# A gated attention block and a routed expert layer in one kernel: routing a block sooner, norms on ScalarE, and a new order of the start

## The reference

```python
x = layernorm(x0)                       # x0: (8, 512, 128), float32; no scale, eps 1e-5
# attention: a second layernorm (with ln_w, ln_b), then
uv = silu(xn @ uv_w.T + uv_b)           # u: 256, v: 256, base: 128 columns
q, k = rope(base * gamma[i] + beta[i])  # i = 0, 1
kern = square(relu(q @ k.T / sqrt(128) + w[j - i + 63]))   # index clipped to 0..126
attn = (u * (kern @ v)) @ o_w.T + o_b + x
# expert layer on x, N = 4096 rows, 8 experts, top 2
probs = sigmoid(x @ W_router); top-2, weights normalised to sum 1
ffn = sq_relu(x @ W_sh_up) @ W_sh_down + sum_e combine[:, e] * (sq_relu(x @ W_up[e]) @ W_down[e])
out = x0 + attn + ffn
```

## Time and profile before

| | |
|---|---|
| median of 3 runs | 433.27 us (432.76 to 434.15) |
| profiled execution | 432.69 us, of it 430.5 us span |
| mean granted clock of TensorE | 0.954 of full speed |
| PE / DVE / ACT / POOL busy | 369.2 / 238.2 / 227.2 / 151.2 us |
| turns 0 to 6 end on PE | 222.3 us |
| first send, last send landed | 139.4, 239.4 us |
| slot tiles on PE | 241.8 to 400.6 us |
| turn 7 and final sums | 401.1 to 430.5 us |

### The profile page before, as it was taken

The page is one execution under the profiler, slowest core; times in us unless marked ns, Lnnn a source line. Parts: engine busy times, 40 slices in busy tenths (PEclk is TensorE's granted clock), DMA queues, the critical chain, the costliest instruction groups (busy, mean ns, idle before and its releaser), DMA issues.

```text
span 430.5 us, 7290 instructions
## 1 busy us (share of the span) xinstructions
PE 369.2 (86%) x1970; PEld 280.1 (65%) x1971; DVE 238.2 (55%) x622; ACT 227.2 (53%) x421; POOL 151.2 (35%) x150
## 2 busy tenths in 40 slices
PE   1557899999899879989950499999999999999992
PEld 1345468676465636646520399999999999999840
DVE  3668877377988858758440133333333333333677
ACT  0354373675466635576520176666666666666520
POOL 3005220000000776764677024444444444444300
PEclk9989899999999998999995599999999999999997
DMA  6929800000000122146111112121212221211397
GB/s 142 266 71 273 177 0 2 1 0 2 0 0 2 45 68 94 46 131 203 45 50 50 50 46 70 56 68 56 68 56 68 56 68 50 74 56 43 108 293 210
DMA packets 50310, 34.00 MB, mean 79 GB/s; under 512 B 5876, under 2 KB 46708, under 8 KB 50293
## 3 DMA queue, kind: packets, MB, share of 16 engines
q1 hardware_dynamic: 43538, 23.71, 21.9%
q0 software_dynamic: 4352, 8.99, 6.3%
q10 hardware_dynamic: 2402, 1.10, 1.1%
HBM read 17.83 MB, written 15.95 MB: 78 GB/s over the span
## 4 chain that ended last, share of the span: by engine, by line
PE 44%; issue 23%; DMA 13%; POOL 8%; DVE 3%; ACT 0%; DVEq 0%; ACTq 0%; SPq 0%
PE bank L1269 15%; DMA slots_in<-work,slot_i 12%; POOL slots_in L982 8%; PE bank L1250 8%; PE bank L1004 5%; PE bank L1005 5%; PE bank L1006 5%; PE bank L1105 3%; PE bank L1243 2%; PE bank L1091 1%; DVE x_all L810 1%; DVE x_all L808 1%; PE bank L1068 1%; DMA slot_x<-slots_in 1%; PE bank L1040 0%
## 5 line engine op out<-in xcount | busy, mean ns | idle before, releaser
L982 POOL DMA_INDIRECT slots_in<-work,slot_i x64 | 68.0, 1062 | 113.8 <-issue 93.3
L991 POOL DMA_INDIRECT results<-work,dest x72 | 69.3, 963 | 95.8 <-DVE work L919 93.0
L1269 PEld LDWEIGHTS bank<-wdn,work 128*128 128x128 f32 x576 | 75.1, 191 | 6.0
L1269 PE MATMUL bank<-wdn,work 128*128 x576 | 75.7, 274 | 0.0
L919 DVE TENSOR_SCALAR work<-bank,row_sum 128x128 f32<-128x128 f32 x72 | 25.2, 350 | 84.0 <-PE bank L1269 82.1
L1105 PE MATMUL bank<-kern,v 128*128 128x512 f32 x128 | 60.3, 606 | 0.0
L592 ACT ACTIVATE work<-bank 128x512 f32<-128x512 f32 x72 | 43.3, 601 | 16.2 <-PE bank L1250 16.0
L598 ACT ACTIVATE work<-bank 128x512 f32<-128x512 f32 x72 | 43.1, 598 | 8.5 <-PE bank L1006 3.1
L586 ACT CAST sx_hi<-bank 128x128 fp32r<-128x128 f32 x72 | 19.0, 266 | 48.5 <-PE bank L1243 48.1
L1250 PE MATMUL bank<-cst,work 128*128 128x128 f32 x288 | 43.9, 275 | 0.0
L1105 PEld LDWEIGHTS bank<-kern,v 128*128 128x128 f32 x128 | 23.5, 197 | 22.0 <-issue 22.0
(11 more groups left out here) (162 smaller groups left out, 657.7 us busy)
## 6 DMA issues: line engine op xcount, KB each, us to landing
slots_in<-zeros SPq DMA_DIRECT2D x1, 4752.0 KB, 22.5
slot_x<-slots_in SPq DMA_DIRECT2D x36, 132.0 KB
work<-in_L_ffn_W_up SPq DMA_DIRECT2D x8, 256.0 KB, 3.1
wdn<-in_L_ffn_W_down SPq DMA_DIRECT2D x4, 512.0 KB, 7.4
wup_hi<-results SPq DMA_DIRECT2D x8, 256.0 KB, 5.1
wup_lo<-results SPq DMA_DIRECT2D x8, 256.0 KB, 5.2
out<-x_all SPq DMA_DIRECT2D x8, 256.0 KB, 3.1
results<-work,dest POOLq DMA_INDIRECT x72
```

What stands on the lines that cost most here:

```text
L982: pool.indirect_dma_start(slots_in, bass.IndirectOffsetOnAxis(slot_i[:, k, t:t + 1], 0), xs1[:, t, at], None, element_offset=k * 2).then_i ...
L991: pool.indirect_dma_start(results, bass.IndirectOffsetOnAxis(dest[:, at:at + 1], 0), slot_y[:, k, :], None).then_inc(returned[k], 16)
L1269: last = pe.matmul(P_Y[h][:, 0:D], hid_t[:, h, rows], wdn[:, of, c, :].rearrange("p a d -> p (a d)"), start=(c == 0), stop=(c == HC - 1))
```

## The change

- The routing's groups 1 to 4 are turned in turn 0 and 5 to 7 in turn 1, logits 0 to 3 in turn 0 and 4 to 7 in turn 1; the DVE pieces each stand one turn earlier (`routing_first`, `_second`, `_weights` in turn 1, `_counts`, `_tiles`, `_slots` in turn 2, `_owners` in turn 3).
- The norms of groups 1 to 7 are 28 activations on ACT (`norm`, with `shift` = -mean x inverse made on POOL) in place of 28 DVE operations. DVE keeps the norm of group 0.
- W_up is split two experts a turn in turns 3 to 6.
- `rotate_sum` of the next block stands at the end of a turn, ahead of `gate`, and not behind it.
- The start: DVE norms block 0 ahead of the uv-bias work, the first rows' parts come ahead of the second's on ACT, and on PE the gates and shared products of block 0 stand ahead of its value part; `output_weights` comes later. SP's loads stand in another order and take over the four small column loads from ACT's queue.
- The score bias: `w` is loaded to 128 partitions, POOL's four copies work on 128 partitions in place of one, 128 equal rows (512 KB) go to DRAM, and the readback starts one element less far in each row, so that it needs neither matmuls nor ACT's copies.

```diff
-            sp.dma_start(w_sb[:, :], w.rearrange("(a n) -> a n", a=1)).then_inc(ld["w"], 16)
+            sp.dma_start(w_sb[:, :], w.rearrange("(a n) -> a n", a=1).broadcast_to([P, WREL])).then_inc(ld["w"], 16)
             load_rows(0, 0, FIRST)
-            load_rows(1, FIRST, 12)
...
+            load_rows(1, FIRST, 12)
+            cols(uvb_c[:, 0:2], uv_b[0:EU].rearrange("(a p) -> p a", p=P))
...
+            sp.dma_start(cos_sin[:, :, :], consts[:, C_COS:C_W].rearrange("p (a t) -> p a t", a=2)).then_inc(ld["cos_sin"], 16)
             sp.dma_start(vb_bc[:, :], uv_b[EU:2 * EU].rearrange("(a e) -> a e", a=1).broadcast_to([P, EU])).then_inc(ld["wide"], 16)
+            load_rows(2, 12, 20)
             sp.wait_ge(ld["dist"], 16)
-            sp.dma_start(bias_t[:, :], bass.AP(by_distance.tensor, by_distance.offset, [[1, P], [1, BIAS_W]])).then_inc(ld["bias"], 16)
+            shifted = bass.AP(by_distance.tensor, by_distance.offset + P - 1, [[2 * T - 1, P], [1, BIAS_W]])
+            sp.dma_start(bias_t[:, :], shifted).then_inc(ld["bias"], 16)
...
+            def norm(g):
+                act.wait_ge(shift_made, {1: 1, 2: 2, 3: 2, 4: 2}.get(g, 3))
+                for t in range(g * TB, g * TB + TB):
+                    last = act.activation(xs1[:, t, X0:X0 + D], x_all[:, t, :], ACT.Identity, bias=shift[:, t:t + 1], scale=inv1[:, t:t + 1])
+                last.then_inc(xs1_act, 1)
...
 (ACT, turn)
+                if 3 <= route < LAST:
+                    weights_hi(2 * route - 5)
+                    weights_hi(2 * route - 4)
                 shared_relu(b, 2)
                 shared_relu(b, 3)
+                if route == 0:
+                    norm(1)
+                    norm(2)
+                    routing_copied(1)
                 if not last:
                     second_rows_hi(b + 1)
...
 (DVE, turn)
                 if 0 < b < LAST:
                     gate(b - 1)
-                if not first:
-                    rotate_sum(b)
-                    v_bias(b)
+                v_bias(b)
                 qk_split(b)
...
                 if route == 1:
-                    first_norm(6)
-                    first_norm(7)
+                    routing_first()
                 if route == 2:
-                    routing_first()
+                    routing_counts()
                 if route == 3:
-                    routing_counts()
-                if route == 4:
                     routing_owners()
...
                 if not last:
                     rotate_base(b + 1)
                     first_rows_lo(b + 1)
+                    rotate_sum(b + 1)
...
 (POOL)
+            pool.wait_ge(var_made, 3)
+            root(inv1, var_eps, slice(FIRST, 8))
+            mean_shift(slice(FIRST, 8), 3)
+            pool.wait_ge(var_made, 4)
+            root(inv2, inv2, slice(FIRST, 8))
+            root(inv1, var_eps, slice(8, 20))
+            mean_shift(slice(8, 20), 5)
```

More of the change, by code:

```diff
@@ L814, in turn @@
                     gate(b - 1)
-                if not first:
-                    rotate_sum(b)
-                    v_bias(b)
+                v_bias(b)
                 qk_split(b)
                 if route == 0:
-                    variances(slice(FIRST, 20))
-                    dve.wait_ge(bias_kept, 2)
-                if route == 1:
-                    first_norm(5)
+                    statistics(2, 12, 20)
+                    dve.wait_ge(ld["bias"], 16)
                 kernel_square(b, 0)
@@ L826, in turn @@
                 if route == 0:
-                    first_norm(1)
-                if not last:
+                    variances(slice(FIRST, 20))
+                elif not last:
                     second_norm(b + 1)
@@ L1026, in value_bias @@
                 pe.matmul(banks[6][:, 0:EU], lnb_bc, uvt_v, start=True, stop=True).then_inc(uv_bias_mm, 1)
-            def score_bias():
-                pe.wait_ge(ld["cst"], 16)
-                pe.wait_ge(ld["bias"], 16)
-                pe.wait_ge(ow_made, 1)
-                for n in range(2):
-                    pe.matmul(banks[4 + n][:, 0:BIAS_W // 2], cst[:, C_REV:C_REV + P],
-                              bias_t[:, n * (BIAS_W // 2):(n + 1) * (BIAS_W // 2)], start=True, stop=True).then_inc(bias_turned, 1)
             def routing_logits(g):
@@ L1135, in turn, with gates, first_up @@
             def turn(b, first, last, route):
+                def gates():
+                    uv_part("u0", b, 0)
+                    uv_part("u1", b, P)
+                def first_up():
+                    pe.wait_ge(x1_lo_made, START + b + 1)
+                    if first:
+                        pe.wait_ge(w_lo_made, 1)
+                    shared_up(b, 0)
+                    if route == 1:
+                        routing_turned(6)
+                    shared_up(b, 1)
+                if first:
+                    gates()
+                    first_up()
                 v_part(b, 0)
@@ L1178, in turn @@
                     output_turned(b - 1)
+                if first:
+                    pe.wait_ge(ow_made, 1)
                 values(b, 0)
+                if route == 0:
+                    routing_turned(1)
+                    values(b, 1)
                 if not last:
@@ L1183, in turn @@
                     routing_logits(1)
-                if route == 1:
-                    routing_turned(6)
-                values(b, 1)
+                    routing_turned(2)
+                    values(b, 2)
+                else:
+                    values(b, 1)
                 if not last:
```

283 lines of the change are left out of this document (131 added, 152 removed).

## The result

The changed kernel takes 403.41 us (median of 4 runs, 401.9 to 406.25) against 433.62 for the kernel before on the same chip (4 runs, 432.76 to 434.15): a ratio of 0.931, 95% interval 0.926 to 0.937. The forecast was 401 us, and faster by 32; it is faster by 30. The profiled execution took 402.98 us, with a span of 401.2.

The account below looks back on a forecast made before the run. Two chains, GpSimd's sends and TensorE's turns, bound the experts' start; both come near 210.8 us against 241.83, 31.0 sooner, plus 1 us of clock: span 398.5, 400.7 with what lies around it, so 401 us; own range 394 to 408, wider range 392 to 411.

Parts of the forecast that it names:

- a race of two chains: Ahead of the experts: the sends, starting when slot_i is made, against TensorE's turns; before, the sends lose by 18.8 us.
- the sends: 64 indirect DMAs from 106.8 us, 101.6 us long (between 100.0 and 103.2), ending at 208.4; first slots there at 210.8.
- the sum: At the experts' start: both chains come at 210.8 against 241.83, 31.0 us sooner; with 1 us of clock, span 398.5.
- the start: Up to block 0's qk_hi on ScalarE: at 25.8 instead of 32.68, ended by o_b, a gain of 6.9 us.
- Turn 0: From block 0's qk_hi to block 1's value part: unchanged at 27.1 us, 1 less to 3 more; value part at 52.9.
- Turn 1: Block 1's to block 2's value part: 27.6 us instead of 30.3, with fewer logits and one group less to turn.
- Turn 2: Block 2's to block 3's value part: 26.4 us, as turn 3 before with its stall; slot_i at 105.6, first send 106.8.
- Turns 3 to 6: TensorE's turns without ScalarE's waits for W_up: 74.8 us for turns 3 to 5, 28.1 for turn 6.
- The clock: At the experts' start: with no long idle TensorE needn't begin at a low clock, 1 us of a possible 0 to 2.
- slower sends: Rival at the sends: slower than 1.61 us each, TensorE waits again, total 409 to 416 us; chance 0.09.
- the slower case: Rival at the start: GpSimd's copies cost by the partition, ahead of the first root; kernel some 595 us; chance 0.03.

Follow-up runs that it names:

- the last version: Changed kernel, one send in flight, with x's first four tiles loaded ahead of w and routing weights one turn later: 404.7 us, ratio 0.934 to the kernel before.

## Why the prediction was right, step by step

Right were the mechanism (a race of two chains to the experts, in which the sends still come last), the side, and the size: 28.7 us of the sum's 31.0 at the experts' start. That the places up to the first send came within 0.5 us is in part luck: the start came 1.7 us sooner than forecast, turns 1 and 2 took 1.3 us longer.

- *The start*: `qk_hi` was forecast at 25.8, ended by `o_b`. It came at 24.08, and what ended it was not `o_b`:

```profile
23.81 0.37 ACT L438 COPY ow<-bank 128x256 f32<-128x256 f32 x1 [1.55 <-PE bank L1024]
24.08 1.05 ACT L514 CAST qk_hi<-work 128x1024 fp32r<-128x1024 f32 x1
```

  The copy of the output weights, which ScalarE takes first, waited for its transposes, and VectorE's rotation ended at 23.2. `o_b` was issued at 14.70 and landed 7.8 us later, at 22.5; only with the single-partition bias did it end the wait, at 23.3. That wait was taken from a load of before, with the bytes added on top; the load landed no later for them.
- *Turn 0*: 27.1 forecast, 27.14 measured. The balance held in sum by luck, as its parts were off and the same code took 26.5 to 28.5 us with the clock. ScalarE's norm is no 266 ns copy:

```profile
49.70 4.75 ACT L443 ACTIVATE work<-x_all,shift,inv 128x128 f32<-128x128 f32 x12
```

  0.40 us each, so 6.4 us for 16 where 4.3 was reckoned; with them on VectorE the turn is 1.2 to 1.3 us shorter.
- *Turn 1*: 27.6 forecast, 27.88 measured.
- *Turn 2*: 26.4 forecast with a stall of 2.14 us; 27.38 with one of 3.14, and 28.9 to 29.0 in the versions in which the clock falls behind it. `slot_i` 105.6 forecast, 105.19 measured; first send 106.8 against 106.3.

```profile
85.63 0.50 PE L1007 MATMUL bank<-x_lo,uvw_hi 128*128 128x512 f32 x1 [3.14 <-DVE work L772]
```

- *The sends* are the term that was mis-sized: 101.6 us forecast between bounds of 100.0 and 103.2, 104.4 measured (106.3 to 208.25 + 2.48). The loads of weights fall among the first 50 sends in both kernels, and these took 81.8 us against 80.7 before, 1.1 us more. The last 14 took 22.6 us to the last landing, which is the 1.61 us each of the upper bound (22.5); before, with the other engines idle, they took 19.3. The middle between the bounds took them as half quiet, and they were not quiet at all.

  Part of it is seen on GpSimd itself. With no operation of VectorE beside it no send takes over 0.96 us there (182 sends in the 14 traces), and each of the 258 that take over 1.0 us has one beside it. The longest, of 1.8 to 2.0 us, all have an operation of VectorE on 128x1024 elements beside them, such as this one (GpSimd, VectorE):

```profile
111.81 1.93 POOL L985 DMA_INDIRECT slots_in<-work,slot_i  x1 [0.34 <-DMA slots_in<-work,slot_i]
```

```profile
111.70 1.21 DVE L766 TENSOR_TENSOR qk_lo<-work,qk_hi 128x1024 fp32r<-128x1024 f32 x1
```

  Other sends beside VectorE's work take 0.96 us too, so not every operation does it. In the changed kernel the excess over 0.96 us is 8.8 us in 64 sends, some of it hidden behind the wait for the send before. From send to send it is 1.44 us in the first 30 of the version without loads and 1.29 in the last 14 of before, with one in flight and no loads in both, so 0.15 us each for the work of the other engines. By the rule of the Trainium skill ("DMA: Bandwidth & Descriptors", SWDGE vs HWDGE vs iDMA), that VectorE's two-port operations keep GpSimd from writing descriptors, the last 14 sends were to lose their quiet, and the traces agree that they did (1.55 us each against 1.29). Whether it is this lock that they wait for no trace shows.
- *Turns 3 to 6*: 25.6, 24.6, 24.6 and 28.1 forecast; 25.07, 23.66, 23.65 and 29.3 measured. No wait of ScalarE for W_up is left in the waits, and its old split brings 10.8 us of it back. The turns were done at 208.1 instead of 209.8, so TensorE lost by 5.0 us and not by 1.
- *The clock*: 1 us was to be won by a shorter idle, with no low clock at the experts' start. This step did not hold: the first transposes of the slots take 0.69 us, and the clock is 0.50 for the first 4 us. Nor is a short idle enough to keep it up. In the seven traces with an idle of 1.8 us the first transposes take 0.43, but in six of them the clock then falls to 0.50 within 4 us. The stretch from the first slot tile to the end took 188.7 us before and 188.1 now, so 0.6 us were won there.
- *The sum*: the experts start 2.3 us later than forecast (2.8 us of sends, less the 0.5 by which the first one came sooner), and 0.4 us of the stretch behind are missing; the span is 401.2 against 398.5.
- *The rivals*: slower sends was the nearest, at 1.63 us each and not 1.7. GpSimd's copies, on which the slower case hung, cost on 128 partitions what they did on one (0.55):

```profile
4.93 0.56 POOL L952 COPY wdn<-w_sb 128x449 f32<-128x449 f32 x1 [4.50 <-DMA w_sb<-in_L_attn_w]
```

  The load of `w` for them delays x's first rows, which costs nothing as long as ScalarE's table load comes last at the start, and 1.2 us when it doesn't.

## What to carry to other kernels

Where two chains race to one point, work out both to the end and give the gain of the change as far as the second chain lets it: here the routing a turn sooner was worth 18 to 20 us, and the split of W_up, which shortened turns 3 to 6 by 3.0 us, moved the experts' start by 2.7 at most and the total by less than can be told. Indirect DMAs that go out one behind the other take longer beside plain loads, and longer too beside the other engines' work, so size each stretch of them by a stretch of before that has the same beside it, and not by a mean. And a version that is fastest on one chip is to be run on another before it is kept: the one with two sends in flight took 400 us on one and 438 on the next.

## What the runs showed of the hardware that was not expected

With a send from GpSimd every 1.3 us and almost no pause, the other engines can come nearly to a stop: in four traces (two in flight three times, one without loads) operations started up to 22 us behind the end of what they waited for, from 147 or 155 us on, until the sends were over. The experts then start 35 to 42 us later than in the undisturbed run with two in flight, and 25 us later than in the changed kernel in the run without loads. In the seven traces of the changed kernel and its versions with one send in flight and the loads beside it (25.6 us of waits in the changed kernel, 19.0 in the last version), and in two with two in flight on another chip, it didn't come. What it is has not been settled. The sends' pattern of the first 30 is the same with and without it (1.433 us each in both runs of one version), so the pace alone doesn't decide it. Nor does the chip alone: the version without loads had it on the chip on which three versions with the loads had not. One send in flight with the loads beside it, the changed kernel's way, was not run on the chip where the three versions had it, so it is not shown that this way keeps free of it everywhere.

The other is the clock behind a short stall: after 3.1 us without work TensorE's clock fell in four traces and held in three, for the same 3.1 us, at a price of 1.6 us; after 1.2 us, at the same place, it held in all six; after 5.0 us it was low in both traces of the changed kernel. In turn 0, around a stall of 1.9 us ahead of block 0's scores, it fell in nine traces and held in three. Part of the scatter of equal kernels lies here.
